# First attention: row sums made from halves that POOL adds; totals rounded and inverted in two halves

## The reference, cut to what matters

```python
qkv = x @ W_qkv + b_qkv
q, k, v = jnp.split(qkv, 3, axis=-1)          # then 16 heads of 16
coef = jnp.einsum('bhqd,bhkd->bhqk', q_h, k_h) / scale
coef = jnp.where(causal[None, None], coef, -jnp.inf)
attn = jax.nn.softmax(coef, axis=-1)          # all in bf16
att_h = jnp.einsum('bhqk,bhkd->bhqd', attn, v_h)
```

## Time and profile before

| | us |
|---|---|
| median of 3 runs | 2035.05 (2033.52 to 2035.66) |
| the profiled execution | 2035.23 |
| its span | 2033.3 |
| DVE busy in the span | 1320.4 (65%) |
| ACT busy | 934.8 (46%) |
| POOL busy | 211.2 (10%) |
| PE busy | 1577.5 (78%) |

### The profile page before, as it was taken

The page is one execution under the profiler, slowest core; times in us unless marked ns, Lnnn a source line. Parts: engine busy times, 40 slices in busy tenths (PEclk is TensorE's granted clock), DMA queues, the critical chain, the costliest instruction groups (busy, mean ns, idle before and its releaser), DMA issues. The chain is left out here.

```text
span 2033.3 us, 33699 instructions
## 1 busy us (share of the span) xinstructions
PE 1577.5 (78%) x9152; PEld 840.1 (41%) x9152; DVE 1320.4 (65%) x4019; ACT 934.8 (46%) x2016; POOL 211.2 (10%) x185
## 2 busy tenths in 40 slices
PE   3555555632199999999999466999999999973995
PEld 1121222211167777777776242333333333331564
DVE  4788888856445555555556496877788878635543
ACT  3888888950011111111111342777777777723212
POOL 0000000000111211111120200111111111101000
PEclk9555555555599999999999686999999999976998
DMA  2255565551100000000000031111111111020001
GB/s 83 51 105 101 101 103 104 107 101 23 29 22 14 27 14 27 14 24 16 16 16 1 17 118 52 32 33 33 34 35 33 35 34 36 16 58 19 1 1 42
DMA packets 197985, 87.81 MB, mean 43 GB/s; under 512 B 166288, under 2 KB 182672, under 8 KB 197840
## 3 DMA queue, kind: packets, MB, share of 16 engines
q1 hardware_dynamic: 196624, 84.30, 18.2%
q10 hardware_dynamic: 1216, 2.03, 0.4%
HBM read 35.29 MB, written 13.24 MB: 24 GB/s over the span
## 5 line engine op out<-in xcount | busy, mean ns | idle before, releaser
L833 DVE CUSTOM_DVE_ANT_0 a_unread<-a_row,all_mask 128x512 bf16<-128x512 f32 (+3 forms) x768 | 392.8, 555 | 106.7 <-PE a_row L678 97.2
L785 ACT ACTIVATE a_probs<-a_st 128x512 f32<-128x512 f32 (+3 forms) x768 | 329.3, 495 | 181.1 <-PE a_st L702 135.2
L1222 PE MATMUL moe_gu<-all_xT_bf,moe_parts 128*112 128x512 bf16 x1536 | 344.9, 382 | 17.8 <-POOL moe_parts L1047 17.8
L1259 ACT ACTIVATE moe_th<-moe_gu 112x512 f32<-112x512 f32 x128 | 76.4, 597 | 489.1 <-PE moe_gu L1222 489.1
L678 PE MATMUL a_row<-l_k,a_q 128*128 128x512 bf16 (+3 forms) x768 | 249.0, 341 | 43.3 <-DMA a_q<-in_q_tail 29.2
L1222 PEld LDWEIGHTS moe_gu<-all_xT_bf,moe_parts 128*112 128x112 bf16 x1536 | 201.1, 131 | 147.3 <-POOL moe_parts L1047 17.9
L699 PE MATMUL a_st<-a_q,l_k 128*128 128x512 bf16 (+3 forms) x768 | 250.7, 333 | 12.3 <-ACT a_probs L785 10.8
L1275 DVE SCALAR_TENSOR_TENSOR moe_tmp<-moe_th,moe_gu 112x512 f32<-112x512 f32 x128 | 88.1, 688 | 255.1 <-ACT moe_th L1259 244.0
L1236 PE MATMUL moe_dn<-moe_wd,moe_actT 112*128 112x256 f32 x1024 | 231.4, 379 | 0.0
L1236 PEld LDWEIGHTS moe_dn<-moe_wd,moe_actT 112*128 112x128 f32 x1024 | 194.7, 190 | 30.2
L544 DVE CUSTOM_DVE_ANT_0 a_rows<-a_sc,all_mask 128x128 bf16<-128x128 f32 (+7 forms) x256 | 192.5, 752 | 14.3 <-PE a_sc L467 13.8
(11 more groups left out here) (202 smaller groups left out, 1684.3 us busy)
## 6 DMA issues: line engine op xcount, KB each, us to landing
a_turned_sb<-a_rows SPq DMA_TRANSPOSE x256, 2.6
moe_raw<-in_gate SPq DMA_DIRECT2D x16, 224.0 KB, 3.0
moe_raw<-in_up SPq DMA_DIRECT2D x16, 224.0 KB, 3.3
moe_wd<-in_down SPq DMA_DIRECT2D x16, 224.0 KB, 2.6
a_q<-q_rows SPq DMA_DIRECT2D x96, 32.0 KB, 2.0
q_rows<-qkv_parts SPq DMA_DIRECT2D x4, 768.0 KB, 3.5
k_rows<-qkv_parts SPq DMA_DIRECT2D x4, 768.0 KB, 3.5
l_k<-k_rows SPq DMA_DIRECT2D x64, 48.0 KB
```

What stands on the lines that cost most here:

```text
L785: nc.scalar.activation(probs[:, n % PR, 0:w], st[:, n % AHEAD, 0:w], ACT.Exp).then_inc(exp_done, 1)
L833: nc.vector.tensor_tensor_reduce(out=unread[:, i % SLOTS, 0:w], in0=row[:, i % SLOTS, 0:w], in1=mask[:, at:at + w], scale=1.0, scalar=-3e3 ...
L1222: last = nc.tensor.matmul(gu[0:IC, n % 2, i, :], parts[:, j, k // KC, i, k % KC, ch * IC:(ch + 1) * IC], xT[:, k % KC, g * 512:(g + 1) * 512],
```

## The change

POOL gets a new step for each item: it adds the left half of the row of exponentials to the right half, in f32, into one of three buffers `halves`. ACT's total_of then sums w / 2 columns of `halves` instead of w columns of `rows`, waits for POOL (`halved`) instead of its own exponential, and runs two items behind the exponential instead of one. POOL's copy of v moves into the order of the adds. DVE rounds and inverts the totals in two halves of eight: the first at item 0 of its pass, the second at item 6; scale(n) stands at its own place from item 1 on, and scale of item 0 behind the first inversion.

```diff
--- before.py
+++ after.py
@@ -403,6 +403,8 @@
 NI = len(ITEMS)
 TURNED = 8
 LAG = 5
+HALVES = 3
+SIDE0 = S // 2
 
 
 def rounded_attention(nc, units, hd, q_rows, k_rows, v_units, att, mask, ident_b):
@@ -417,6 +419,7 @@
         v_sb = c.sb("v", [P, 2, TB, 2 * hd], BF16)
         rows = c.sb("rows", [P, 2, COLS], BF16)
         unread = c.sb("unread", [P, 2, S], BF16)
+        halves = c.sb("halves", [P, HALVES, SIDE0], F32)
         turned_sb = c.sb("turned_sb", [P, TURNED, TB, P], BF16)
         mx = c.sb("mx", [P, 2, NI], BF16)
         total = c.sb("total", [P, 2, NI], F32)
@@ -424,9 +427,9 @@
         inv = c.sb("inv", [P, 2, NI], F32)
         sc = c.ps("sc", [P, 3, 2, 512], F32)
         o = c.ps("o", [P, 2, 512], F32)
-        names = ("sc_ready", "maxed", "less_max", "exp_done", "summed", "inv_ready", "p_ready", "pv_done", "o_copied", "v_ready")
+        names = ("sc_ready", "maxed", "less_max", "exp_done", "summed", "inv_ready", "p_ready", "pv_done", "o_copied", "v_ready", "halved")
         (sc_ready, maxed, less_max, exp_done, summed, inv_ready, p_ready, pv_done, o_copied,
-         v_ready) = (c.sem(n) for n in names)
+         v_ready, halved) = (c.sem(n) for n in names)
         turned = [c.sem(f"turned{i}") for i in range(TURNED)]
         qk_loaded = (c.sem("qk_loaded0"), c.sem("qk_loaded1"))
         block = ctx.enter_context(nc.Block())
@@ -503,10 +506,10 @@
                 u, e = n // NI, n % NI
                 qb, h, at = ITEMS[e]
                 w = (qb + 1) * P
-                act.wait_ge(exp_done, n + 1)
+                act.wait_ge(halved, n + 1)
                 if n >= 2:
                     act.wait_ge(summed, n - 1)
-                nc.scalar.activation(unread[:, n % 2, 0:w], rows[:, u % 2, at:at + w], ACT.Copy,
+                nc.scalar.activation(unread[:, n % 2, 0:w // 2], halves[:, n % HALVES, 0:w // 2], ACT.Copy,
                                      accum_out=total[:, u % 2, e:e + 1]).then_inc(summed, 1)
 
             def finish(u):
@@ -516,10 +519,11 @@
 
             for n in range(total_items):
                 exp(n)
-                if n:
-                    total_of(n - 1)
+                if n >= 2:
+                    total_of(n - 2)
                 if n % NI == LAG + 1 and n // NI >= 2:
                     finish(n // NI - 2)
+            total_of(total_items - 2)
             total_of(total_items - 1)
             finish(units - 2)
             finish(units - 1)
@@ -527,10 +531,27 @@
 
         @block.gpsimd
         def _(pool):
-            for u in range(units):
+            def halve(n):
+
+                u, (qb, h, at) = n // NI, ITEMS[n % NI]
+                w = (qb + 1) * P // 2
+                pool.wait_ge(exp_done, n + 1)
+                if n >= HALVES:
+                    pool.wait_ge(summed, n - HALVES + 1)
+                nc.gpsimd.tensor_tensor(out=halves[:, n % HALVES, 0:w], in0=rows[:, u % 2, at:at + w],
+                                        in1=rows[:, u % 2, at + w:at + 2 * w], op=ALU.add).then_inc(halved, 1)
+
+            def copy_v(u):
                 if u >= 2:
                     pool.wait_ge(pv_done, NI * (u - 1))
                 nc.gpsimd.tensor_copy(v_sb[:, u % 2], v_units[:, u]).then_inc(v_ready, 1)
+
+            copy_v(0)
+            copy_v(1)
+            for n in range(total_items):
+                halve(n)
+                if n % NI == LAG + 3 and n // NI >= 2:
+                    copy_v(n // NI)
 
         @block.vector
         def _(dve):
@@ -553,14 +574,15 @@
                 dve.wait_ge(maxed, n + 1)
                 nc.vector.tensor_scalar(row, row, mx[:, u % 2, e:e + 1], None, ALU.subtract).then_inc(less_max, 1)
 
-            def total_rounded(u):
-                dve.wait_ge(summed, NI * (u + 1))
-                nc.vector.tensor_copy(totb[:, u % 2], total[:, u % 2]).then_inc(inv_ready, 1)
-
-            def inverse(u):
-                dve.wait_ge(inv_ready, 2 * u + 1)
-                nc.vector.reciprocal(inv[:, u % 2], totb[:, u % 2]).then_inc(inv_ready, 1)
-                dve.wait_ge(inv_ready, 2 * u + 2)
+            def total_rounded(u, first, end):
+                dve.wait_ge(summed, NI * u + end)
+                nc.vector.tensor_copy(totb[:, u % 2, first:end], total[:, u % 2, first:end]).then_inc(inv_ready, 1)
+
+            def inverse(u, first, end):
+                done = 4 * u + (2 if first else 0)
+                dve.wait_ge(inv_ready, done + 1)
+                nc.vector.reciprocal(inv[:, u % 2, first:end], totb[:, u % 2, first:end]).then_inc(inv_ready, 1)
+                dve.wait_ge(inv_ready, done + 2)
 
             def scale(n):
                 u, e = n // NI, n % NI
@@ -577,16 +599,19 @@
                     ahead = n + NI < total_items
                     if ahead:
                         maximum(n + NI)
-                    if e == 1:
-                        total_rounded(u)
-                    if e >= 2:
+                    if e == 0:
+                        total_rounded(u, 0, NI // 2)
+                    if e == NI // 2 - 2:
+                        total_rounded(u, NI // 2, NI)
+                    if e:
                         scale(n)
                     if ahead:
                         less(n + NI)
-                    if e == 1:
-                        inverse(u)
-                        scale(n - 1)
+                    if e == 0:
+                        inverse(u, 0, NI // 2)
                         scale(n)
+                    if e == NI // 2 - 2:
+                        inverse(u, NI // 2, NI)
 
 
 def attention(nc, tag, units, hd, m_row, dt, q_load, k_load, loads, k_sb, v_units, o_rows, mask, late, ident_b):
```

## The result

The changed kernel takes 2098.82 us (median, 2097.07 to 2101.84) beside 2035.3 us for the kernel before (here the median of four runs): a ratio of 1.0315 (95% interval 1.0298 to 1.0333), 3.2% slower. Its profiled execution has a span of 2095.2 us, 61.9 us longer than before.

A forecast was written before the change was run, and what follows sets the result against it. It took DVE's work and its wait for ACT's last sum as the bound, SyncE's queue close behind. Fifteen passes +64.2 us, first unit +2, last unit -3.3, together +63 on 2035.2: 2098 us, range 2031 to 2128.

The forecast's parts named there:

- What bounds the kernel before: First attention's loop, 23.98 us a pass (one unit): DVE's 2.8 us wait for ACT's last sum; SyncE's queue next at 23.4.
- no-hold case: Rival: adds hold DVE for nothing, SyncE's queue bounds the loop at 23.4 us a pass, 2021 us; chance 0.16.
- Second rounding and inversion: On DVE, one more cast and one more inversion of totals in each pass: +0.37 us a pass.
- The wait: DVE's standing still for ACT's last sum of a unit, 2.8 us each, was to go.
- Each hold: A POOL add waiting behind DVE's scaling delays the following subtraction by the add's duration less 0.26 us.
- The sum of the holds: Twelve of sixteen adds cost DVE 7.2 us, the small ones 0.2: 7.4 us a pass.
- Which instruction is held: Adds of the twelve wider items become ready inside DVE's scaling and get in ahead of the subtraction, which pays.
- The pass: One unit of the first attention's loop: DVE's 20.6 + 0.37 + 7.4 = 28.35 us; fifteen passes +64.2 us.
- The first unit: Its maxima and subtractions, 17.34 us before, meet adds too: +2 us, at most 3.6 + 0.9.
- the random phase: Rival: adds fall at random on TENSOR_SCALARs, 3.9 us of holds a pass, 2045 us; holds in part or at random 0.20.
- a hold of 0.2 us whatever the add's length: Rival: holds fixed at the copies' 0.2 us, 3.2 us a pass, about 2036 us; within the 0.20 case.
- late totals: Rival: totals still come late, so DVE's wait of up to 2.8 us a pass stays, 2140 us; chance 0.04.

The follow-up runs named there:

- e1: The kernel before with only the rounding and inversion of the totals split into two halves of eight, no adds on POOL: ratio 0.9944, 2027.24 us.
- e7: The kernel before with its four loads of q and k a unit issued from ACT's queue instead of SyncE's: ratio 1.000, 2036.19 us.
- e9: The kernel before with totals rounded in two halves and one double-width DMA transpose for two heads, no adds on POOL: ratio 0.9893, 2013.54 us.
- e2: The changed kernel with every POOL add cut to 2 columns, all instructions and semaphores kept, totals wrong: ratio 0.9947, 2026.97 us.
- e4: The changed kernel with each POOL add also waiting until DVE has subtracted the next item, so it starts with a maximum: ratio 0.9958, 2029.67 us.
- e3: The kernel before plus the same 256 POOL adds, whose result nobody reads; ACT still sums all columns: ratio 1.0441, 2127.58 us.
- e5: The changed kernel with every POOL add half as wide, ACT still summing half the columns, totals wrong: ratio 1.0024, 2041.39 us.

## Why the prediction was right

It put the time at 2098 us; 2098.82 was measured. The term that decides, the holds, was right in its rule and its size, though not in which instruction is held. That the total agrees within 1 us is in part luck, as the last steps show. Step by step:

- *What bounds the kernel before*: right. DVE's wait for ACT was the removable part (e1: -0.6%; e7: unloading SyncE alone does nothing), and SyncE's queue stood close behind (e1, e9). Its bound was put at 23.4 us a pass and is 23.6, so the no-hold case ends at 2027 (e1, e2) and not at 2021.
- *Second rounding and inversion*: 0.37 us a pass was put. DVE's busy time rose by (291.54 - 288.07)/14 = 0.25 us in e1, which has this part alone.
- *ACT*: 17.7 us a pass, as worked out. *The wait*: gone.
- *The adds' own length*: 1.16 us for 512 columns from 0.19 us and 1.89 ns a column; those that need not wait for a TENSOR_SCALAR take 1.15 to 1.17 (e4), those of 64 columns 0.30 for 0.31.
- *Each hold*: 0.89 us behind a scaling for 0.90 predicted.
- *The sum of the holds*: 7.4 us a pass was predicted, 7.5 measured, and the parts agree too if each hold is put down to the add that it overlaps: the twelve adds of 192 to 512 columns cost 7.3 us a unit where 7.2 had been put, the four of 64 and 128 columns 0.2 as predicted. By the width of the instruction that is held it looks otherwise: those of 384 to 1024 columns lose 6.5 us, and the subtraction of 128 columns takes 664 ns instead of 252, because an add holds an instruction of a later item, and the last add of 512 columns one of the next unit.
- *Which instruction is held*: only in part as predicted. The prediction has every wide add become ready inside a scaling, so that the subtraction behind it pays. 36.4 of the 119.6 us lie on the scalings. In four of the sixteen items of a pass (both of 512 columns, the first of 896 and of 1024) the add starts within 0.03 us of the scaling and holds that, as at 301.43 and 301.44 above, there for 0.83 us where 0.78 had been put. The price is nearly the same, so the sum doesn't show it. The last add of a unit had been priced at 0.90 us without following it into the items of 128 columns, where it lands; that it cost as much there (1.18 - 0.25 us) is luck. e3 shows how it could have gone: there the same add falls into a wait and costs nothing.
- *The pass*: 28.2 us for 28.35; over fifteen passes, +62.1 us for +64.2.
- *The first unit*: +5.5 us. I took +2 and bounded it at 4.5. ACT is busy only 14.90 of the 22.82 us there once it sums half the columns, so it doesn't lag, and toward the end both adds of a width hold a subtraction and not one of them: the last two, of 1024 columns, take 1.19 and 1.42 us. The bound of 4.5 us was wrong.
- *The end*: between the last subtraction and the first transpose of the last unit lie 0.6 instead of 4.0 us (from 503.38 to 504.01, before from 436.47 to 440.45), -3.4 for -3.3.
- *The rest of the span*: 2.3 us shorter than before, 0.7 us before this stage and 1.7 us behind the first transpose of its last unit; the predicted sum had nothing for it, and the cause is open. With the 2.1 us of the passes it hides the first unit's miss of 3.5: 62.1 + 5.5 - 3.4 - 2.3 = 61.9.

The rivals: no hold at all is refuted by the change and shown by e2 to be what short adds would have given; the random phase (2045 us) is refuted by the order of time and by 7.5 instead of 3.9 us of holds; a hold of 0.2 us whatever the add's length by e2, where adds of 237 ns cost nothing, and by the 0.89 us above; late totals by the one wait of 0.7 us. The point of 3.0 us a pass from which the change loses is a little lower, since 3.1 us (e5) already lose 0.2%. The Trainium skill's rule ("SBUF — State Buffer", section "Who interferes with whom") that the loser is blocked for the whole instruction agrees: the 0.20 us between release and the add's recorded end are a constant, and the hold grows with the add from 0.14 us beside a copy to 0.89.

## What to carry to other kernels

Before moving work to POOL, look in the trace at the DVE instructions that run at that time: here the TENSOR_SCALARs, which read and write bf16 in SBUF, stood still until 0.20 us before the end of POOL's copy or add, and POOL got in between two of them; the maximum, which reads PSUM, lost nothing. Price each meeting from the order of time (when the POOL instruction becomes ready, what DVE is doing then), not from POOL's busy share. If the work must stay, try to make it wait for the start of a DVE instruction that reads PSUM and is as long. And ask what comes next behind a wait that you remove: here it was a DMA queue at 1.3 us a transpose. Halving the count of transposes, with the new order of the totals and more distance between issue and use, brought 55 us where the change cost 63.

## What the hardware showed beyond the expected

- A DMA transpose costs its queue nearly the same at any width up to 1024 columns (1.12 us for 128, 1.29 for 1024) and more beyond (1.9 us for 2048), so one wide transpose is cheaper than two of half its width.
- POOL's add takes 0.30 us for 64 and 1.15 to 1.17 us for 512 columns with bf16 inputs and f32 output, no faster a column than f32 inputs (1885 ns for 896).
- A DVE instruction of 0.25 us can cost 1.18 us: the price is set by what POOL runs, not by what DVE runs.
